# A Mamba, FFN and attention block: the lower half of the FFN becomes a thread of its own, with new instruction orders

## The reference, cut to what matters

```
x = x + 0.5 * ffn(norm(x))           # "front": fp4-quantised linear layers, 256 -> 704 -> 256
x = x + mamba(norm(x))               # "head" (projections, conv, dt, gate) and "scan" (16 states, 512 steps)
x = x + 0.5 * ffn(norm(x))           # "back": the same FFN weights
x = x + 0.5 * lora_linear(norm(x))   # routed LoRA layer
x = x + attention(norm(x))           # 16 heads, ALiBi, causal
x = x + 0.5 * lora_linear(norm(x))

def ffn(x):
    h = silu(fp4(x) @ fp4(w_gate).T) * (fp4(x) @ fp4(w_up).T)
    return fp4(h) @ fp4(w_down).T
```

## Time and profile before

| | us |
|---|---|
| median of 3 runs | 4851.23 |
| lowest and highest | 4837.85 and 4863.45 |
| the profiled execution's own time | 4869.6 |
| its span | 4867.8 |
| VectorE busy | 4003.6 |
| TensorE busy | 3920.1 |
| ScalarE busy | 2382.9 |
| POOL busy | 1616.1 |

### The profile page before, as it was taken

How to read it: one execution, slowest core, us unless ns; L and a number is a source line. 1 busy time by engine, 2 the same in 40 slices (tenths; PEclk the granted TensorE clock), 3 DMA queues, 4 the chain that set the end, 5 groups by cost and what they waited for, 6 DMA issues and landing times.

```text
span 4867.8 us, 52570 instructions
## 1 busy us (share of the span) xinstructions
PE 3920.1 (81%) x17423; PEld 1994.1 (41%) x17452; DVE 4003.6 (82%) x5964; ACT 2382.9 (49%) x4341; POOL 1616.1 (33%) x1036
## 2 busy tenths in 40 slices
PE   4466777888888888888797988879897887978777
PEld 2123343443435444343444443434444343534343
DVE  6587898898998989799787989889897988988622
ACT  2343454545555554555455464546555454555332
POOL 0143433332433334242333343334333342424200
PEclk8677788898989989899998989989898898988787
DMA  1577787667587766777567686677759668667300
GB/s 57 140 170 173 163 203 161 167 154 173 147 183 174 174 159 161 164 165 161 143 156 188 135 200 161 159 180 157 197 112 217 153 142 193 151 175 177 92 23 28
DMA packets 241427, 753.30 MB, mean 155 GB/s; under 512 B 37650, under 2 KB 132659, under 8 KB 171524
## 3 DMA queue, kind: packets, MB, share of 16 engines
q1 hardware_dynamic: 241156, 749.95, 65.1%
HBM read 647.30 MB, written 101.71 MB: 154 GB/s over the span
## 4 chain that ended last, share of the span: by engine, by line
PE 45%; DVE 29%; ACT 8%; DMA 7%; issue 6%; POOL 3%; SPq 2%; DVEq 0%; ACTq 0%; POOLq 0%
DVE state L1680 6%; PE m L1149 6%; PE m L1179 6%; DVE mt L1777 4%; DVE u L1675 3%; PE pd L1389 3%; PE y L1249 3%; PE m L1195 3%; DMA state<-dtx_scratch 2%; POOL state L758 2%; PE y L1262 2%; DVE front L1613 2%; PE m L1212 1%; DMA gz_scratch<-front 1%; PE pu L1365 1%
## 5 line engine op out<-in xcount | busy, mean ns | idle before, releaser
L758 POOL TENSOR_TENSOR state<-state,bc 128x1024 f32<-128x1024 f32 x512 | 1233.8, 2410 | 1716.2 <-DVE u L1675 1703.6
L1680 DVE TENSOR_TENSOR_SCAN state<-decay,u 128x1024 f32<-128x1024 f32 x512 | 1167.3, 2280 | 16.2 <-ACT decay L949 7.2
L1149 PE MATMUL m<-w_gu,hats_m 128*128 128x480 f32 (+1 forms) x1536 | 720.0, 597 | 60.1 <-DVE front L1591 40.4
L949 ACT ACTIVATE decay<-decay,a_neg 128x511 f32<-128x511 f32 x1024 | 675.5, 713 | 142.6 <-DMA decay<-dt_scratch 142.0
L1675 DVE TENSOR_TENSOR u<-state,bc 128x1024 f32<-128x1024 f32 x512 | 641.6, 1253 | 49.3 <-DMA state<-dtx_scratch 40.3
L1249 PE MATMUL y<-state,sel 128*32 128x512 f32 x2048 | 312.1, 687 | 214.4 <-POOL state L758 210.4
L1179 PE MATMUL m<-w_dn,front 128*128 128x256 f32 (+1 forms) x1536 | 441.7, 426 | 22.6 <-ACT front L883 21.9
L1149 PEld LDWEIGHTS m<-w_gu,hats_m 128*128 128x128 f32 x1536 | 284.9, 200 | 347.4 <-issue 194.1
L742 POOL TENSOR_TENSOR front<-front,hsc_m 128x704 f32<-128x704 f32 x128 | 193.0, 1508 | 688.4 <-DVE front L1496 688.4
L1179 PEld LDWEIGHTS m<-w_dn,front 128*128 128x128 f32 (+1 forms) x1536 | 294.6, 207 | 139.5 <-issue 56.2
L1195 PE MATMUL m<-hats_m,w_in 128*128 128x512 f32 x512 | 282.1, 676 | 54.0 <-DVE front L1649 17.9
(11 more groups left out here) (261 smaller groups left out, 7046.6 us busy)
## 6 DMA issues: line engine op xcount, KB each, us to landing
decay<-dt_scratch SPq DMA_DIRECT2D x256, 1024.0 KB, 7.3
state<-dtx_scratch SPq DMA_DIRECT2D x256, 1024.0 KB, 11.4
qk_scratch<-shared SPq DMA_DIRECT2D x64, 384.0 KB, 5.2
shared<-qk_scratch SPq DMA_DIRECT2D x384, 64.0 KB
kh<-qk_scratch SPq DMA_DIRECT2D x384, 64.0 KB
xs_scratch<-front SPq DMA_DIRECT2D x16, 1024.0 KB, 6.5
dt_scratch<-front SPq DMA_DIRECT2D x256, 64.0 KB, 5.9
dtx_scratch<-hats_m SPq DMA_DIRECT2D x256, 64.0 KB, 4.8
```

The source lines that it names most:

```text
L758: eng.tensor_tensor(st, st, bc[:, 1:2, :].to_broadcast([P, WIDE, L]), ALU.mult).then_inc(scan_pool.sem, scan_pool.step(f"c{r}{h}"))
L949: ins = eng.activation(d, d, ACT.Exp, scale=a_neg[:, g:g + 1])
L1149: mm = eng.matmul(f.bank(f"gu{t}{p}")[:, 0:2 * width], norm.hat_t[:, k, t * P:(t + 1) * P], w_gu[:, k, 2 * lo:2 * (lo + width)], start=(k ...
L1680: eng.tensor_tensor_scan(st, decay[:, n % ND, h * WIDE * L:(h + 1) * WIDE * L], u[:, :], 0.0, ALU.mult, ALU.add).then_inc(scan_dve.sem, sc ...
```

## The change

- `weave` gets a fifth generator, `fifth`, which runs `low` for every FFN. On PE `low` holds the transposes and the down product, on ACT the copies `ht{t}a`, `ht{t}b` and `res{t}`. On SP, POOL and DVE it is empty. Thread 0 keeps the rest. Two new semaphores, `low_pe` and `low_act`, carry the events of these steps.
- All five strings of `ORDER` are new.
- ACT's waits for the stores of the heads before (`xs_saved`, `dt_saved`, `gz_saved`) move from ahead of the copies of the transposed input (`evac_hat`) to the first tanh of the FFN.
- Each norm gets its own `pause` tile.
- `keep` and `KEEP` go; zero products are now a sixth generator, `keeper`, that the PE string could call with the digit 5.
- `f.uses`, the buffers and the instructions themselves stay.

```diff
-                self.pe = Steps(sem(f"ffn_pe_{tag}"), ["x0", "x1"] + gu(0) + [
-                    n for t in range(T) for n in (gu(t + 1) if t < T - 1 else []) + [f"ht{t}a", f"ht{t}b", f"dn{t}"]])
+                self.pe = Steps(sem(f"ffn_pe_{tag}"), ["x0", "x1"] + [n for t in range(T) for n in gu(t)])
+                self.low_pe = Steps(sem(f"low_pe_{tag}"), [n for t in range(T) for n in (f"ht{t}a", f"ht{t}b", f"dn{t}")])
...
+            def fifth():
+                for w, n in FFNS:
+                    yield from low(FFNS.index((w, n)), n)
...
-            weave(order, first(), second(), third(), ahead())
+            weave(order, first(), second(), third(), ahead(), fifth(), *idle)
...
@@ ACT @@
             def ffn(front, r, n):
-                x = xx[:, n % NX, :, :]
-                yield
-                heads = heads_before(r)
-                if heads:
-                    eng.wait_ge(xs_saved, 16 * heads)
-                    for b in range(2):
-                        eng.wait_ge(dt_saved[b], 128 * heads)
-                        eng.wait_ge(gz_saved[b], 32 * heads)
+                yield
                 yield from evac_hat(f.act, r, f.pe, normed("front" if front else "back", n)[0].hat_t, (f.bank("x0"), f.bank("x1")))
...
                         yield
+                        heads = heads_before(r)
+                        if t == 0 and p == 0 and heads:
+                            eng.wait_ge(xs_saved, 16 * heads)
+                            for b in range(2):
+                                eng.wait_ge(dt_saved[b], 128 * heads)
+                                eng.wait_ge(gz_saved[b], 32 * heads)
...
+            def low(r, n):
+                x = xx[:, n % NX, :, :]
+                for t in range(T):
                     for part, (lo, hi) in (("a", (0, 4)), ("b", (4, IK))):
                         yield
...
-                    yield
-                    eng.wait_ge(f.pe.sem, f.pe.after(r, f"dn{t}"))
-                    eng.activation(x[:, t, :], f.bank(f"dn{t}")[:, 0:D], ACT.Copy).then_inc(f.act.sem, f.act.step(f"res{t}"))
+                    yield
+                    eng.wait_ge(f.low_pe.sem, f.low_pe.after(r, f"dn{t}"))
+                    eng.activation(x[:, t, :], f.bank(f"dn{t}")[:, 0:D], ACT.Copy).then_inc(f.low_act.sem, f.low_act.step(f"res{t}"))
...
@@ PE @@
-                yield from gate_up(0)
                 for t in range(T):
-                    if t < T - 1:
-                        yield from gate_up(t + 1)
+                    yield from gate_up(t)
+
+            def low(r, n):
+                for t in range(T):
                     down = f.bank(f"dn{t}")
...
-            run(ORDER["PE"], lead, ffn, head, scan, lora, attention)
+            run(ORDER["PE"], lead, ffn, low, head, scan, lora, attention, keeper())
```

More of the change, by code:

```diff
@@ L231, in weave @@
         next(threads[int(n)], None)
-    assert all(next(t, "end") == "end" for t in threads)
+    assert all(next(t, "end") == "end" for t in threads[:THREADS])
 def build(nc, a, out):
@@ L500, in heads, with run @@
             return att_bank[event][:, 0:n * width].rearrange("p (g l) -> p g l", g=n)
-        def run(order, lead, ffn, head, scan, lora, attention):
+        def run(order, lead, ffn, low, head, scan, lora, attention, *idle):
             def first():
@@ L765, in attention @@
                 yield from rstd(nr, q)
-            run(ORDER["POOL"], lead, ffn, head, scan, lora, attention)
+            run(ORDER["POOL"], lead, ffn, low, head, scan, lora, attention)
         @block.scalar
@@ L1036, in attention @@
                                    ).then_inc(att_act.sem, att_act.step(f"res{b}"))
-            run(ORDER["ACT"], lead, ffn, head, scan, lora, attention)
+            run(ORDER["ACT"], lead, ffn, low, head, scan, lora, attention)
         @block.tensor
@@ L1115, in banks_free, with free @@
                     else:
[L1116 removed]
+                        eng.wait_ge(f.low_act.sem, f.low_act.after(FFNS.index((user, m)), f"res{T - 1}"))
+            def free(r, use):
+                before = f.uses.index(use) - len(f.banks)
+                if before >= 0:
+                    user = f.uses[before]
+                    if user[0] == "x":
+                        eng.wait_ge(f.act.sem, f.act.after(r, user))
+                    elif user[0] == "g":
+                        eng.wait_ge(f.dve.sem, f.dve.after(r, f"h{user[2:]}"))
+                    elif user[0] == "h":
+                        eng.wait_ge(f.low_act.sem, f.low_act.after(r, f"{user}a"))
+                    else:
+                        eng.wait_ge(f.low_act.sem, f.low_act.after(r, f"res{user[2:]}"))
             def ffn(front, r, n):
[L1119 removed]
+                norm = normed("front" if front else "back", n)[0]
                 yield
[L1121 removed]
                 eng.wait_ge(f.lead_dve.sem, f.lead_dve.after(r, "rescaled"))
@@ L1199, in head @@
                     yield
-                    keep(f"in{m}")
                     if m == 0:
@@ L1785, in attention @@
                             yield from divide(int(w[2]))
-            run(ORDER["DVE"], lead, ffn, head, scan, lora, attention)
+            run(ORDER["DVE"], lead, ffn, low, head, scan, lora, attention)
 def constants():
```

379 lines of the change are left out of this document (172 added, 207 removed).

## The result

The changed kernel takes 4686.25 us in the median of four runs (4671.84 to 4694.46) where the kernel before took 4852.04 beside it: a ratio of 0.9656 with a 95% interval of 0.9621 to 0.9692, 3.4% less. The forecast was 4802, 1.0% less, with 4705 as the low end.

The account below looks back on a forecast made before the run. Short waits between threads, seen as VectorE's 468.7 us idle in the steady stretch, were taken to bound the kernel; the terms summed to -49 us, 4869.6 to 4820.6, scaled to 4802 us; range 4705 to 4905.

Parts of the forecast that it names:

- the waits -5: ACT: moving the store waits to the first tanh spares PE's waits for x copies, -5 us, bounds -18 and 0.
- VectorE's order. This is where the time is decided: VectorE, steady stretch: each wait priced by the other threads' work covering it in both strings, at step durations of before.
- Tanh to `s`, -13: VectorE, steady stretch: the 59.8 us wait for tanh falls through fewer short covers, -13 us, bounds -30 and 0.
- `up` after `size`, +15: VectorE, FFN tiles 1 to 3: cover shrinks from 4.8 to 2.5 us, +15 us, bounds 0 and +72.
- The rival that has `size` late: ACT, tiles 1 to 3: answers of about 3.1 us and more expose 72 us, scaled time 4895 us; chance 0.20.
- `rec` -20, back statistics -15, `log` -10: VectorE, steady stretch: waits in attention (42.3 us), back FFN (38.0) and head (37.4) fall by 20, 15 and 10.
- The attention thread's starts, -10: VectorE: waits for lg, va and stats_r (14.8, 15.0, 15.5 us) fall by 10 us, bounds -30 and 0.
- Start, 0: VectorE's work ahead of the first scans is nearly the same in both strings: 0 us, bounds -15 and +30.
- VectorE beside POOL, +5: VectorE: 15 more small steps stand close behind u, beside POOL products; +5 us, 9 at most.
- End +4: After the last scan: VectorE's work grows from 122 to 126 us, +4 us.
- SP 0: SP's new string: late loads cost VectorE 24.6 us in the steady stretch; change 0 us, bounds -25 and +25.
- Larger gain: FFN chain up to 269 us shorter; with even covers takes a third of 469 us idle, scaled 4707 us; chance 0.15.

Follow-up runs that it names:

- e1: The changed kernel's code with the five order strings of the kernel before, so every engine keeps the old order: 4851.01 us, ratio 0.9993.
- e7: The changed kernel with `size` put back behind `res` on ScalarE in 82 of 96 places: 4934.6 us, ratio 1.0178 to the kernel before.
- e2: The new code in the old order, with only `size` put ahead of `res` in all 96 places: 4838.33 us, ratio 0.997 to the kernel before.
- e13: e7 with 265 steps of other threads put ahead of `up` on VectorE, in 73 of 78 places: 4844.59 us, ratio 0.998 to the kernel before.
- e8: The changed kernel with gate/up's first half put back behind down on TensorE in 56 of 64 places: 4764.01 us, ratio 0.9829 to the kernel before.
- e10: The changed kernel's code in the author's third layout, threads 0 and 4 tied in the old sequence: 4816.96 us, ratio 0.9925 to the kernel before.
- e12: The changed kernel's layout with some 900 single steps moved a few places, nothing put back: 4898.01 us, ratio 1.0069 to the kernel before.
- e3: The changed kernel's code in a first layout from the author's list scheduler, five threads: 4878.57 us, ratio 1.0041 to the kernel before.
- e5: The changed kernel's code in a second scheduler layout reckoning with the loads' queue, five threads: 5055.2 us, ratio 1.0395 to the kernel before.
- e11: The changed kernel's layout with `size` and gate/up put back in 140 places, then some 900 small moves: 5027.24 us, ratio 1.0346 to the kernel before.
- e9: The changed kernel's code in a third layout keeping two-SBUF-input VectorE steps off GpSimd's products, five threads: 4793.66 us, ratio 0.9878 to the kernel before.

## Why the prediction was right or wrong

**Right:** the reading of what bounds the kernel. The gain is VectorE's idle time and nothing else (188.8 of 197.8 us), the work is the same, and zero products, the new semaphores and the moved waits are worth nothing that e1 can tell (I had given the waits -5, within what e1 can't tell). `up` stayed under 55 us (12.7), `rec`, `log` and the back statistics fell below their rows, the end is within 10 us of 308. One sign missed: tanh was to stand near 100 us in all, and has 61.5.

**The step that failed** is "*VectorE's order. This is where the time is decided*". I counted the cover of each wait in both strings, and set it against the answers' durations of before. But the fifth thread shortens the answers themselves (`size` by 3.3 us in the mean of the 96 tiles), and the new order is laid out for the short ones. I saw that ("2.8 us earlier", 269 us "from the FFN's own chain") and set it aside with "it is not the gain: VectorE filled the hole with a scan part". e7 shows what it is worth in the new order: without it that order waits 275 us for `size` and loses 248. e2 and e13 hint that the hole is not filled for free either: where a wait for `size` was taken away or covered, other groups waited longer, though little more than traces differ.

**And half of the gain had no term.** I priced the waits that the earlier trace rows show, and gave the attention maxima and the head's other steps nothing, without a reason. In the steady stretch the waits that I priced fell by 72 us in all, with the statistics' +53 taken in, and those that I did not price by 76. No run parts what made these fall.

- *Tanh to `s`, -13.* Measured -31 in the steady stretch, -62 over the span, beyond the bound of -30. The mean cover was indeed nearly the same; the answer came sooner. I had found the first half of gate/up ahead of down in 34 of 64 places; counted again by the names of the steps it is all 64, and I gave it no price. e8 gives it: 78 us, all in this wait.
- *`up` after `size`, +15.* Wrong sign: -8 in the steady stretch (11.3 to 3.5), -24.5 over the span. The cover did shrink, but `size` now starts 0.03 us behind `scaled` in the tile above and takes 0.79 us. The rival that has `size` late was reckoned with an answer of 3 us, which was that of the old order.
- *`rec` -20, back statistics -15, `log` -10.* -33, -20 and -21 in the steady stretch: all within their bounds, each larger than taken.
- *The attention thread's starts, -10.* `lg` and `va` gave 6.5 us, but its norm's statistics after L1050 grew from 15.5 to 68.9. Taken together the term came to +47 where I had -10, and its bound above was 0. So the rest gained more than the total says.
- *Start, 0.* Measured -40, outside its bound of -15, though e1 shows that 13 us of it can come from one trace to the next. Tanh and `up` in the first 1000 us, before and then after, went down by 37 together. With the freedom on ScalarE taken away (e7) VectorE's work in these 1000 us is back at 801 us, and `up` waits 45.4 there, so the start too hangs on the freedom.

```profile
DVE front L1587 <- ACT front L864: 41.6, 23, 8.0
DVE front L1493 <- ACT front L870: 23.8, 12, 3.2
```

```profile
DVE front L1576 <- ACT front L875: 23.2, 25, 6.8
...
DVE front L1482 <- ACT front L881: 5.3, 8, 0.9
```

- *VectorE beside POOL, +5.* The small scale step went from 277 to 266 ns, and `up` from 975 to 888 ns, since it is seldom begun inside a product any more: about -13 us, with the sign against me. I counted only the two small kinds, not the passes of 0.89 us.
- *End +4:* the stage is 8 us shorter. *SP 0:* u's loads wait 18.3 where they waited 24.6.

The third rival, *Larger gain*, took "a third of the 469 us", and the steady stretch gave 148 against its 145. That the sizes agree so well is luck: half of the 148 lies in waits that nobody priced. Its reason, that the FFN's chain is shorter, holds for tanh and `up` (e7, e8). It stopped at 4707, 21 us above the measured time, and gave the start nothing.

**How much is the freedom, how much the layout?** In this order the freedom is needed: taking the ScalarE half away costs 248 us, 158 after one mending, and the TensorE half 78. Alone in the old order it is worth 0.3% (e2). A tied layout reached 0.75% (e10). The pairs of one procedure differ by 1.6%, -0.9%, 0.5% and 2.6% in favour of five threads. So neither L nor F alone explains what was measured: by these runs the freedom pays in an order laid out for it, and little outside one. Open stays how near a tied order could come if laid out as well as this one, and that is the question between F and L. My best layouts come to 4817 with the tie and 4794 without, where the changed kernel has 4686, so they can't answer it. Why the statistics after L1050 grew was not tried either.

## What to carry to other kernels

When a change frees a step from an in-order neighbour, price the answer that its consumer now gets, not only the cover that stands in the string: cover spent on a slow answer is cover taken from other waits. Then undo the freedom in the new order, not only grant it in the old: e2 says 0.3%, e7 says 5%, and both are true. And price every wait of the stage, not only those that seem touched by the change: here those without a term gave half of the gain in the steady stretch. A tight order answers badly to small moves that look harmless: some 900 of them cost over 4% (e12).

## What the runs showed of the hardware

Most of VectorE's instructions with two SBUF inputs, and its small scale step, are held up while a scan's product (2.35 us) runs on GpSimd. In the traces of the changed kernel, e1, e3 and e5 those that began inside a product ended a fixed time after the product did, however early they had begun: `scaled`, `up` and `down` 0.75 us after it (by themselves they take 0.89), u 1.09 us after it (1.23), the scale step 0.04 us after it (0.19). So the price of a collision is what the product still has to run: `up` took up to 3.06 us. Those with a PSUM input (L1576, L1580, L1605, L1769), the maximum over one SBUF tile (L1466, 0.89 and 0.89) and the scan (2.29 outside and 2.28 inside a product) are untouched. The Trainium skill (SBUF — State Buffer, "Who interferes with whom") says that VectorE and GpSimd lock each other out at a shared port pair, and that a VectorE instruction with two SBUF inputs contends with a GpSimd instruction that reads SBUF. These runs agree for the first group, of which the earlier trace rows had shown only the smallest member. They differ for the scan, which has two SBUF inputs and is not held up. In a bad order this is worth 107 us of VectorE's time (159 in e5, 52 in the changed kernel).

TensorE's busy time is not fixed: 3920.1 us before, 3881.7 after and 3998.0 in e7, with the same products, at a mean granted clock of 0.877, 0.897 and 0.876. (The first and the last have the same clock and are 78 us apart, so the clock is not all of it.) In the steady stretch the changed kernel had more of the higher level (2.4 GHz), 0.92 where it was 0.90, and kernels that kept TensorE fuller mostly had the higher clock (e8, 82% busy, 0.901; e11, 79%, 0.879). How much of the 3.4% came with the clock was not tried. Two bounds can be read. TensorE's products and weight loads together took 61 us less in the changed kernel's trace, which is about the most that the clock can have given directly. And over 61 executions of the kernel before, the time fell by some 3.5 us for each 0.001 of granted clock; the changed kernel stands 0.018 higher in its median, an estimate of some 60 us if the clock were the cause and not the effect. It can't be the whole: e9 has the changed kernel's clock (0.896) and takes 4794 us.
